# Layer F's first score rows sent earlier, a third bank for its scores, later rows in the accumulator's bank, and the last batch's choices sent by SyncE

## The reference, cut to what matters

```python
x = L0_attn_x                                        # (8, 512, 128)
# layer A: 16 heads of width 8, queries are the normalised x itself
n = layernorm(x); K = n @ Wk + bk; V = n @ Wv + bv
x = x + n + gelu(softmax(causal(Q K^T)) @ V) @ Wf + bf
# layer F: 8 heads of width 64, 8 experts, one chosen per row and head
n = layernorm(x); q = n @ w_q; k = n @ w_k
gates = sigmoid(n @ w_gate); sel = argmax(gates, -1); gm = one_hot(sel, 8) * gates
values = einsum('bhne,ehdk,bnd->bhnk', gm, value_experts, n)
o = softmax(causal(q * 0.125 @ k^T)) @ values
x = x + einsum('bhne,ehkd,bhnk->bhnd', gm, output_experts, o).sum(heads)
```

## Time and profile before

| | us |
|---|---|
| median of 3 runs | 1187.67 (1184.46 to 1187.96) |
| the profiled execution | 1187.65 |
| its span, first to last instruction | 1185.9 |
| TensorE busy | 1120.6, 94% |
| VectorE busy | 863.0, 73% |
| ScalarE busy | 938.4, 79% |
| GpSimd busy | 399.6, 34% |

### The profile page before, as it was taken

One profiled execution on the slowest core, in us unless ns is written; L12 is line 12 of the kernel. 1 busy time (PEld: TensorE's weight loads), 2 busy tenths in 40 slices (PEclk: granted clock), 3 DMA queues, 4 the chain that ended last, 5 costly groups with the idle time before them and its releaser, 6 DMA issues.

```text
span 1185.9 us, 20345 instructions
## 1 busy us (share of the span) xinstructions
PE 1120.6 (94%) x5846; PEld 649.6 (55%) x5846; DVE 863.0 (73%) x2715; ACT 938.4 (79%) x2639; POOL 399.6 (34%) x652
## 2 busy tenths in 40 slices
PE   5999999999999999999999999999999999999998
PEld 3636754476445754357543775447643585436753
DVE  5835868678785878769687687858787596866844
ACT  3995799858996789967999489976899679995751
POOL 1033324523334334342244332452343532432320
PEclk9999999999999999999999999999999999999999
DMA  6321232022220333003320223202231033201130
GB/s 198 74 76 44 52 111 66 5 64 71 84 56 4 73 92 98 13 15 74 105 72 14 54 53 100 66 4 64 84 88 39 4 82 103 80 2 46 39 73 9
DMA packets 43648, 72.75 MB, mean 61 GB/s; under 512 B 9664, under 2 KB 25408, under 8 KB 43216
## 3 DMA queue, kind: packets, MB, share of 16 engines
q1 hardware_dynamic: 42142, 66.95, 21.2%
q10 hardware_dynamic: 1394, 4.50, 1.5%
HBM read 45.34 MB, written 8.80 MB: 46 GB/s over the span
## 4 chain that ended last, share of the span: by engine, by line
PE 65%; ACT 15%; DVE 9%; issue 5%; DMA 2%; POOL 1%; SPq 1%; ACTq 0%; DVEq 0%; POOLq 0%
PE ps_m L731 14%; PE ps_o L711 10%; ACT masked L956 7%; ACT pt L1007 6%; PE ps_max L608 5%; PE ps_exp L610 3%; PE ps_exp L517 3%; PE ps_m L517 3%; PE ps_exp L519 3%; PE ps_exp L518 3%; PE ps_m L519 3%; PE ps_m L518 3%; PE ps_max L610 3%; PE ps_max L611 3%; PE ps_max L848 2%
## 5 line engine op out<-in xcount | busy, mean ns | idle before, releaser
L956 ACT ACTIVATE masked<-masked,low 128x512 f32<-128x512 f32 (+3 forms) x768 | 423.1, 555 | 48.5 <-DVE low L1349 45.9
L1349 DVE CUSTOM_DVE_ANT_0 masked<-ps_max,mask 128x512 f32<-128x512 f32 (+3 forms) x768 | 349.3, 488 | 128.5 <-PE ps_max L608 77.5
L1216 POOL TENSOR_SCALAR_AFFINE_SELECT pt<-pt 128x256 f32<-128x256 f32 (+2 forms) x384 | 181.7, 475 | 477.5 <-ACT pt L1007 477.1
L1007 ACT ACTIVATE pt<-ps_exp 128x384 f32<-128x384 f32 (+1 forms) x400 | 202.1, 518 | 31.0 <-PE ps_exp L611 25.1
L711 PE MATMUL ps_o<-pt,val 128*32 128x128 f32 (+6 forms) x1536 | 178.8, 445 | 6.1 <-POOL pt L1216 5.4
L731 PE MATMUL ps_m<-at,oe_sb 128*128 128x512 f32 x300 | 154.3, 601 | 1.8 <-DVE at L1400 1.8
L956 ACT ACTIVATION_READ_ACCUMULATOR masked<-masked,low 128x1 f32 x768 | 147.5, 192 | 0.0
L608 PE MATMUL ps_max<-s2k,s1q 72*128 72x512 bf16 (+3 forms) x512 | 121.2, 304 | 18.7 <-DVE low L1349 10.6
L1400 DVE TENSOR_TENSOR at<-osb,hots 128x512 f32<-128x512 f32 x150 | 107.0, 714 | 15.9 <-PE ps_m L731 15.8
L610 PE MATMUL ps_exp<-s1q,s1k 128*128 128x256 f32 (+2 forms) x256 | 97.6, 392 | 10.6 <-DVE val L1540 9.5
L711 PEld LDWEIGHTS ps_o<-pt,val 128*32 128x32 f32 (+1 forms) x1536 | 51.7, 117 | 93.4 <-POOL pt L1216 44.6
(11 more groups left out here) (191 smaller groups left out, 2055.6 us busy)
## 6 DMA issues: line engine op xcount, KB each, us to landing
hots<-hot_d SPq DMA_DIRECT2D x48, 256.0 KB, 4.6
s1q<-parts_q SPq DMA_DIRECT2D x96, 96.0 KB
s2k<-parts_k SPq DMA_DIRECT2D x93, 96.0 KB
s1q<-pt SPq DMA_DIRECT2D x64, 128.0 KB, 2.3
s1k<-pt SPq DMA_DIRECT2D x64, 128.0 KB, 2.3
hots<-hot_d ACTq DMA_DIRECT2D x16, 256.0 KB, 4.8
parts_q<-pt SPq DMA_DIRECT2D x24, 128.0 KB, 2.3
parts_k<-pt SPq DMA_DIRECT2D x24, 128.0 KB, 3.9
```

The lines of the kernel that those rows point to most:

```text
L956: last = nc.scalar.activation(e, e, ACT.Exp, bias=low[:, g % 2, c:c + 1], scale=-1.0, accum_out=den[:, g % 2, c:c + 1])
L1007: nc.scalar.activation(pt[:, (n % 2) * 4 + j, 0:c1 - c0], score_bank(k, u)[:, c0:c1], ACT.Exp).then_inc(exp_done[k].sem, 1)
L1216: nc.gpsimd.affine_select(out=v, in_=v, compare_op=ALU.is_ge, fill=0.0, base=0, pattern=[[0, w], [0, m], [1, P]], channel_multiplier=-1).t ...
L1349: last = v.tensor_tensor_reduce(out=masked[:, u % JUNK, c0:c0 + w], in0=src[:, c0:c0 + w], in1=mask[:, S - w:S], scale=-1.0, scalar=POS, o ...
```

## The change

- The transposition of group 0's rows in layer F goes from value 27 to value 24, and ScalarE copies them right after its copy of q/k product 7, ahead of the stack copies of that product.
- Layer F's scores turn through three banks, `ps_m0`, `ps_exp0`, `ps_exp1`. The first three wait for 29, 31 and 32 values.
- The rows of groups 1 to 3 are transposed into bank 1, the accumulator's, instead of bank 0. Product 0 therefore stands at u = 16 at the earliest: the table goes from 14, 15, 16, 17, 19, 20, 21, 22 to 14, 16, 17, 18, 19, 20, 21, 22; for the last batch from two a step in 14 to 17 and eight more in 18 to 23, to two a step in 16 to 23.
- The first rows of layer A go to bank 0 instead of bank 2 and wait for one exponential of layer F fewer.
- In the last batch SyncE sends parts 0 and 1 of the masks ahead of group 1's rows, and ScalarE sends none.

```diff
-SCORE_BANKS = {"A": 3, "F": 2}
+SCORE_BANKS = {"A": 3, "F": 3}
...
-BANK["A", "T", 0] = 2
+BANK.update({("F", "T", g): 1 for g in range(1, GROUPS)})
...
-NEGATE_AT, TRANSPOSE_AT, COPY_AT = 23, 27, 27
+NEGATE_AT, TRANSPOSE_AT, COPY_WITH = 23, 24, 7
...
-STEPS_AT = [("F", 14 + 5 * m // 4) for m in range(OUTPUTS_F)] + [("pre", n) for n in (2, 5, 8, 11)]
+STEPS_AT = [("F", 15 + m if m else 14) for m in range(OUTPUTS_F)] + [("pre", n) for n in (2, 5, 8, 11)]
...
-    OUTPUTS_LAST["F", (14 + m // 2) if m < E else (18 + 3 * (m - E) // 4)].append(m)
+    OUTPUTS_LAST["F", 16 + m // 2].append(m)
...
-            return ps_exp[u % 2]
+            return (ps_m[0:1] + ps_exp)[u % 3]
...
                 if f + 1 == B:
+                    for p in range(2):
+                        repeat_hots(f, p)
                     maxima_rows("F", f, 1)
-                    for p in range(1, GROUPS):
+                    for p in range(2, GROUPS):
                         repeat_hots(f, p)
...
-                    if k == "A" and exp_done["F"].count(b - 1, UNITS["F"] - 1):
-                        pe.wait_ge(exp_done["F"].sem, exp_done["F"].count(b - 1, UNITS["F"] - 1))
+                    if k == "A" and exp_done["F"].count(b - 1, UNITS["F"] - 2):
+                        pe.wait_ge(exp_done["F"].sem, exp_done["F"].count(b - 1, UNITS["F"] - 2))
...
-                    pe.wait_ge(chosen.sem, chosen.count(b, choices(min(T * E - 1 + u, T * E))))
+                    pe.wait_ge(chosen.sem, chosen.count(b, choices(T * E - (3, 1, 0)[u])))
...
-                                for p in HOTS_AT.get(u, ()):
+                                for p in HOTS_AT.get(u, ()) if b + 1 < B else ():
                                     repeat_hots(b, p)
...
+                    if u == COPY_WITH:
+                        maxima("F", f, 0)
                     if u % 2 == 1:
...
-                if n == COPY_AT:
-                    maxima("F", f, 0)
```

## The result

The changed kernel took 1190.9 us in the median of 8 runs (1189.06 to 1196.61), the kernel before, on the same chip, 1187.59 (8 runs, 1184.46 to 1189.26): a ratio of 1.004, with an interval of 1.0028 to 1.0052 (the two medians alone differ by 0.28%). The change makes the kernel slower, by 0.3 to 0.5%. The profiled execution took 1191.61 us, with a span of 1189.9, against 1187.65 and 1185.9 before.

A forecast was written before the change was run, and what follows sets the result against it. TensorE, busy 94% of the span, was taken as the bound, with ScalarE and VectorE pacing each layer's early part. 1187.65 + 4.2 (7 x 0.60, batches 0 to 6) - 2.4 (batch 7) = 1189.4 us; range 1183.0 to 1191.6.

The forecast's parts named there:

- the three cases: Whole kernel against a 0.3% margin: faster 0.25, slower 0.17 and a tail of 0.02, the same 0.56.
- The front: Start of layer F, batches 0 to 6: score 0 1.2 us earlier, of which 0.26 per batch survives.
- either part of the change alone would gain almost nothing: Before score 0: rows land little before the bank's choice ends, so early rows or third bank alone barely help.
- nothing beyond the 0.26: Third bank, scores after group 1's transposition: no further gain, as later transpositions hang on ScalarE and DVE; bounds 0 and 0.3.
- The product: Late layer F: a product now in full step 18 adds 0.86 us between scores 18 and 19; net 0.60 per batch.
- Rival (a): After step 18, batches 0 to 6: ScalarE sets the pace and hides the moved product; 1183.4 us, chance 0.25.
- The lateness: TensorE's 0.60 us per batch from step 18 on, claimed to reach the next layer's value products.
- The step that failed: Step 15, batches 0 to 6: removing product 0's 0.93 us leaves a hole where TensorE waits for DVE anyway.
- Batch 7: Last batch: earlier weighing, -1.75 us, and later products, -0.68, together -2.4.
- The order of products: Last batch: group 3's transposition ahead of the first product, 1.61 us sooner with 0.93 of work owed; 0.68 won.
- The first weighing: Last batch, layer F: weighing starts near 1124.0 instead of 1125.74, counted as -1.75 us.
- Rival (b): Early layer F: ScalarE's wait for group 0's transposition, from about 0.9 us, loses the 0.26; 1191.3 to 1191.8 us, chance 0.17.

The follow-up runs named there:

- The filled kernel: Changed kernel plus one unused product of 0.9 us of TensorE's time in step 15 of batches 0 to 6: 1188.74 us, ratio 1.0017 to the kernel before.

## Why the prediction was right and wrong

The forecast was 1189.4, +1.7 us; measured were 1190.9, +3.3 in the medians, and 1191.61, +4.0, in the profiled execution. It lies in the range, but by the ratio, 0.4%, the change is past the 0.3% that I called no change, and slower was the least likely of the three cases. The forecast said that nothing would be seen, and a loss is seen.

**The front, right in the sum, wrong in the parts.** -0.26 per batch was forecast; negation to transposition 2 is 20.98 before and 20.71 after, -0.27. The path was the one described: score 0 without a gap, then the transposition of group 1 held by VectorE. But score 0 came 0.36 sooner and not 1.2, and three steps under the sum were false. I wrote that "either part of the change alone would gain almost nothing" and gave the bank nothing beyond the 0.26; the bank alone, with what goes with it, brings all of it, although its score 0 still waits 0.67 for rows, and the early rows bring none. As I read the marks: in two banks score 0 waits for a late choice, whether its rows are there or not (7.74 and 7.72); in three it doesn't, starts 0.4 to 0.5 sooner, and what then holds it, its rows or nothing, is hidden by VectorE's work ahead of group 1's transposition. I placed the transposition at 554.3 with no wait, where value 25 ends and not value 24. TensorE in fact waits 0.79 there, which is most of what score 0 lacks of the 1.2; the run at value 25 has score 0 1.30 sooner and gains nothing by it. And the layer doesn't repeat every 139.6 us alike: batch 2 is 0.4 to 1 us longer than most in every profile, and why is not known.

**The product, right.** 0.86 per batch behind score 18 was forecast, +0.85 measured in every batch. In step 15 only 0.09 was won (1.90 against 1.99), so the hole was not closed but left. Rival (a), that this is hidden, falls. The lateness did reach the next layer. Net per ordinary batch: -0.27 - 0.09 + 0.85 = +0.49, against 0.60; 7 x 0.49 = +3.4, against 4.2. The filled kernel, which has these terms and a clock of 1.00 behind step 15, shows +3.3 over its seven periods.

**The step that failed.** "The time of product 0 was time that TensorE waits for DVE anyway; taking it out leaves a hole of that size": for the clock behind that hole the sum has no term, as if it were nothing. Behind it the granted clock falls to 0.50 for 3.4 us in some batches, and each such stretch costs 1.6 (7.09 for 5.49). Two of them in the profiled execution are the missing +3.2; 3.4 + 3.2 = 6.6 stands against the 6.3 found. Over the three profiled kernels with the hole it was 6 batches in 21, or 7 x 6/21 x 1.6 = 3.2 us to be expected; in the six with the old table and no hole there, none in 42. I had the earlier trace rows before me and used them for batch 7 only, where the hole was to shrink, not for the seven batches where the change opens one. The filled hole shows it: same intervals, a clock of 1.00 behind step 15 in all seven batches, 2.7 us less in the ratios. These low stretches follow idle time of 0.37 to 0.40 and 0.27 us. But the same instructions at the same idle fall in two batches and not in five, so these rows could not tell me which; until more is known, its cost belongs in a sum as an expectation.

**Batch 7, half right.** Of -2.4, -1.5 came. The order of products gave -0.7 (forecast 0.68). The first weighing came 0.88 sooner and not 1.75. Of the 1.75, 0.7 stood for the low clock of the earlier trace rows, and no run shows that it is the change that lifts it: behind a wait of 1.51 us before score 0 the clock is 0.52 in the profile before, but behind 1.53 and 1.52 it is 1.00 in those with the last batch's edits alone and with the table alone. 0.65 of the 0.88 is this clock (group 0's negation to the first weighing is 13.00 in the kernel before and 12.35 with the last batch's edits alone). So this part is luck, and not the change's doing for certain. That leaves 0.23 of a forecast 1.05. VectorE's maximum came 0.9 sooner, as I said. But then I let the negation keep its time, and it took 2.1 us, against 1.4 in the profile before, beside GpSimd's product: 0.7 of the 0.9 gone. With the negation quick, GpSimd's values were the next to be late. The sum of the whole, for the profiled execution: from the forecast's +1.7, -0.8 for the batches' ordinary cost, +2.9 for the clock, +0.9 for batch 7 and -0.8 at the start make +3.9, against 4.0. That the median came within 1.5 us of the forecast is luck, as these terms have opposite signs.

**Rival (b)**, ScalarE's wait at 1191.3 to 1191.8, has the right time for the wrong reason: ScalarE waited 0.25 for the transposition, far from the 0.9 at which it would decide. **Open**: why a given batch falls to the low clock and its neighbour doesn't.

## What to carry to other kernels

A filler that stands in a wait is free where it is and costs its full time where the engine is full (here 0.09 us a batch won where it left and 0.85 paid where it went): before moving one, look at what fills the place it leaves and the place it goes to. Here the place it left on TensorE had a second price, the clock behind the hole, 1.6 us in 6 of 21 batches; with a product in the hole it fell there in none of seven, and the kernel took 2.7 us less by the ratios. So try giving TensorE work where it must wait. When a change has several parts, measure each alone; here one part brought all of the gain of batches 0 to 6 and another took more than that away.

## What the runs showed of the hardware that was not expected

- A hole of TensorE in two pieces of 0.37 to 0.40 and 0.27 us idle, in a stretch in which it is otherwise full, was followed in 2 of 7 batches (3 of 7 with the table alone, 1 of 7 with the transposition behind value 25) by 3.4 us of granted clock 0.50, at a cost of 1.6 us each. Filled with a product, it was followed by none in seven (clock 1.00). In batch 7 the same 1.5 us wait was followed by the low clock in one kernel's profile (1.51, the kernel before, clock 0.52 for 3.4 us) and not in two others' (1.52 with the table alone, 1.53 with the last batch's edits alone, clock 1.00).
- Two of VectorE's operations on 128x8 words took 0.58 and 0.96 us while GpSimd ran its two products of 128x512 from and to SBUF (2.04 us), and 0.16 and 0.17 when those were moved behind them.
